# Transformer block on one core: attention products in bursts of sixteen matmuls, projection pieces between the two scores of a pair

## What is computed

```python
mod = (silu(c) @ wmod).reshape(8, 6, 1, 512)          # sa, ca, ga, sb, cb, gb; |ga|, |gb| >= 0.25
h = layernorm(x) * (1 + ca) + sa
q, k, v = ((h @ W + bias).reshape(b, 16, 32, 1024) for each)   # a plain reshape: 64 tokens make one head
attn = softmax(einsum('bhdt,bhds->bhts', k, v) * temperature)  # scores from k and v
x = x + ga * einsum('bhdt,bhts->bhds', q, attn).reshape(b, 1024, 512)
h = layernorm(x) * (1 + cb) + sb
x = x + gb * (h with, for the 512 tokens of the highest router score, sigmoid(score) * ffn(h) added)
```

## Time and profile before

| | |
|---|---|
| median of three runs | 2613.66 us |
| profiled execution, its own time | 2608.22 us |
| its span, first to last instruction | 2606.5 us |
| mean granted TensorE clock, as a share of 2.4 GHz | 0.971 |
| row maxima, L708 on DVE | 1024, 1216 ns each |
| Exp, L598 on ACT | 1024, 1117 ns each |
| qn, L769 on DVE | 257, 643 ns each |

### The profile page before, as it was taken

The page is one execution under the profiler, slowest core; times in us unless marked ns, Lnnn a source line. Parts: engine busy times, 40 slices in busy tenths (PEclk is TensorE's granted clock), DMA queues, the critical chain, the costliest instruction groups (busy, mean ns, idle before and its releaser), DMA issues. The chain is left out here.

```text
span 2606.5 us, 42013 instructions
## 1 busy us (share of the span) xinstructions
PE 2347.0 (90%) x13016; PEld 897.3 (34%) x13016; DVE 2014.1 (77%) x2697; ACT 1498.0 (57%) x2631; POOL 1247.9 (48%) x1103
## 2 busy tenths in 40 slices
PE   7899999999999999999999999991099999999996
PEld 2333333333333333333333333330044444444443
DVE  5899999899899999999999989994456446644632
ACT  1788788788788788878888878871211111111110
POOL 4455555455455545555455545552314535443541
PEclk9999999999999999999999999996599999999998
DMA  6322232232332232223223233226701120112010
GB/s 200 77 70 73 66 96 62 75 81 71 78 82 74 64 90 75 70 67 90 70 75 82 70 79 82 74 63 36 193 18 44 41 61 32 48 40 61 21 53 16
DMA packets 124912, 183.60 MB, mean 70 GB/s; under 512 B 43748, under 2 KB 43748, under 8 KB 124656
## 3 DMA queue, kind: packets, MB, share of 16 engines
q1 hardware_dynamic: 114936, 155.46, 24.5%
q0 software_dynamic: 9728, 25.23, 3.1%
HBM read 68.23 MB, written 43.16 MB: 43 GB/s over the span
## 5 line engine op out<-in xcount | busy, mean ns | idle before, releaser
L708 DVE TENSOR_REDUCE nmax<-sc 128x1 f32<-128x1024 f32 x1024 | 1230.1, 1216 | 131.9 <-PE sc L409 120.1
L598 ACT ACTIVATE probs<-sc,nmax 128x1024 f32<-128x1024 f32 x1024 | 1138.1, 1117 | 337.1 <-DVE nmax L708 319.4
L409 PE MATMUL sc<-stacks 128*128 128x512 f16 x2048 | 615.7, 382 | 80.3 <-ACT probs L598 47.0
L457 PE MATMUL acc<-probs,qn 128*32 128x512 f32 x4136 | 551.8, 606 | 9.8 <-DVE x L746 7.3
L1156 ACT ACTIVATE g<-ff,b_col 128x512 f32<-128x512 f32 x128 | 88.0, 687 | 578.8 <-PE ff L1095 528.4
L409 PEld LDWEIGHTS sc<-stacks 128*128 128x128 f16 x2048 | 155.1, 97 | 612.4 <-ACT probs L598 328.1
L1108 PE MATMUL ff<-w,g 128*128 128x512 f16 x1536 | 352.4, 379 | 14.7 <-DVE g L1205 13.9
L1095 PE MATMUL ff<-fT,w 128*128 128x512 f16 x1536 | 353.8, 381 | 1.6 <-DVE fT L1190 1.6
L1203 DVE CAST g<-g 128x512 f16<-128x512 f32 x128 | 76.9, 601 | 291.1 <-ACT g L1156 243.7
L887 POOL TENSOR_SCALAR k<-kv 128x512 f16<-128x512 f32 x66 | 41.0, 621 | 511.1 <-ACT kv L571 511.0
L1108 PEld LDWEIGHTS ff<-w,g 128*128 128x128 f16 x1536 | 148.8, 98 | 199.2 <-DVE g L1205 21.5
(11 more groups left out here) (127 smaller groups left out, 2178.1 us busy)
## 6 DMA issues: line engine op xcount, KB each, us to landing
stacks<-k SPq DMA_DIRECT2D x528, 64.0 KB, 2.0
stacks<-v SPq DMA_DIRECT2D x528, 64.0 KB, 2.0
xt<-in_L_attn_x SPq DMA_DIRECT2D x140, 128.0 KB, 2.6
h_rows<-hbuf SPq DMA_DIRECT2D x132, 128.0 KB, 2.3
out<-base SPq DMA_DIRECT2D x132, 128.0 KB, 2.5
rows<-mod_rows SPq DMA_DIRECT2D x32, 256.0 KB, 4.1
stage<-in_L_ffn_W SPq DMA_DIRECT2D x8, 1024.0 KB, 9.9
probs<-in_L_wmod SPq DMA_DIRECT2D x4, 1024.0 KB, 10.0
```

Of the source, the lines that this page charges most:

```text
L409: mm = nc.tensor.matmul(slot(g, v)[:, half * D:(half + 1) * D], stacks[g % 2][:, 0, hq, i * P:(i + 1) * P], stacks[g % 2][:, 1, hq, half * ...
L457: mm = nc.tensor.matmul(acc[at:at + DH, :], qn[:, (p // 2) % 2, p % 2, h2, :], probs[:, (2 * p + h2) % PROBS, half * D:(half + 1) * D], st ...
L598: nc.scalar.activation(probs[:, u % PROBS, :], slot(g, ring_at(p, h2)), ACT.Exp, bias=nmax[:, u % PROBS:u % PROBS + 1], accum_out=rsum[:, ...
L708: nc.vector.tensor_reduce(nmax[:, u % PROBS:u % PROBS + 1], slot(g, ring_at(p, h2)), AX.X, ALU.max, negate=True).then_inc(max_done, 1)
```

## The change

PE's order within a pair becomes: score tile 0, projection piece, score tile 1. Behind score tile 1 of every odd pair p the products of the pairs p - 3 and p - 2 follow as one burst of 16 matmuls. The wait for `qn` stands ahead of the burst, once for both, and so does the wait for the free accumulator (at p = 3 and 11, where it was at 4 and 12). The waits of the pieces for `kv_evac` and `q_evac` move with the pieces. The prologue's product counts 2 on `pv_done` where it counted nothing, since the burst of pair 1 now completes the pairs 14 and 15 of the group before. Behind the loop two pairs of products remain, not four. DVE reads `acc` at the pairs 2 and 10, where it did at 3 and 11.

```diff
-            products(NQ)
+            products(NQ).then_inc(pv_done, 2)
...
                         scores_of(b, g, p, 0)
-                        pe.wait_ge(qn_done, b * (GB * PAIRS // 2) + g * (PAIRS // 2) + p // 2 + 1)
-                        if p in (LAG, LAG + NQ):
-                            pe.wait_ge(acc_free, b * (GB * SUBS) + g * SUBS + (p - LAG) // NQ + 2)
-                        products((p - LAG) % PAIRS).then_inc(pv_done, 1)
-                        scores_of(b, g, p, 1)
                         if p < 12:
                             if p % 3 == 0:
...
                             whole(piece)
+                        scores_of(b, g, p, 1)
+                        if p % 2 == 1:
+                            pe.wait_ge(qn_done, b * (GB * PAIRS // 2) + g * (PAIRS // 2) + (p + 3) // 2)
+                            if p in (3, 3 + NQ):
+                                pe.wait_ge(acc_free, b * (GB * SUBS) + g * SUBS + p // NQ + 2)
+                            products((p - 3) % PAIRS).then_inc(pv_done, 1)
+                            products((p - 2) % PAIRS).then_inc(pv_done, 1)
...
-            for p in range(PAIRS, PAIRS + LAG):
-                pe.wait_ge(qn_done, B * (GB * PAIRS // 2) + (p - PAIRS) // 2 + 1)
-                products(p - LAG).then_inc(pv_done, 1)
+            pe.wait_ge(qn_done, B * (GB * PAIRS // 2) + 2)
+            for p in (PAIRS - 2, PAIRS - 1):
+                products(p).then_inc(pv_done, 1)
...
                         row_max(b, g, p, 0)
-                        if p == 3:
+                        if p == 2:
                             gated(b, g - 1, 1)
-                        if p == 11:
+                        if p == 10:
                             gated(b, g, 0)
```

## The result

The changed kernel takes 2785.31 us (median of 4 runs, 2782.34 to 2789.47) where the kernel before takes 2614.34: a ratio of 1.065 [1.063, 1.068]. The forecast was 2692, with a range of 2635 to 2750. It was slower, as forecast, but by 171 us and not by 78.

A forecast was written before the change was run, and what follows sets the result against it. PE was taken to bound ordinary pairs, the copies of v after the fourth evacuation the group's end. 2.44 us more in each of 32 groups, 78 us on 2608.2, gave 2686, scaled to the median 2692; range 2635 to 2750.

The forecast's parts named there:

- 95 or more: Sign of being right: PE's bias matmul waits for ACT's evacuation at p = 3 and 9, 95 us or more in all.
- piece 0 to piece 9: Group stretch from the projection piece of p = 0 to that of p = 9: 29.03 us against 26.74 before.
- p = 2, 3: Burst to burst over these pairs, with PE waiting 1.46 us for bank pj at p = 3: 7.30 us.
- p = 6, 7: Burst to burst over these pairs, with the piece starting at 2.99: 6.50 us, before 6.08.
- the piece of p = 9: Piece released after DVE's late statistics and aggregation delay the evacuation: 6.18 us from the start of the burst ahead.
- the rule on weight loads: Burst: loads run beside matmuls only if row groups differ; would cost some 0.2 more per burst, forecast some 40 us higher.
- rival 2: Much slower: qn comes late in most rounds because POOL holds it up; 2759 us, chance 0.13.
- the sum for one group: First score to fourth evacuation of an attention group: 40.42 us against 37.98, so 2.44 us more per group.
- From the first score to piece 0 it is 0.52: Start of a group: the first projection piece follows the first score by 0.52 us, where it was 2.07.
- the round of p = 4 and 5: Burst to burst over these two pairs: 5.54 us, before 5.66.
- Behind the fourth evacuation I keep the 15.11: End of a group: GpSimd split and DMA copies of v up to the next first score stay at 15.11 us.
- could cost up to 1 us a group: End of a group: extra cost if PE's and DVE's two rounds, 13.6 to 15 us, don't fit the 15.11.

The follow-up runs named there:

- the early evacuation: Changed kernel with each k/v slice in two pieces at the first two of its three pairs, evacuated in the second: 2614.0 us, ratio 1.002.
- the cut subtract: Changed kernel with GpSimd's subtract of 2.13 us cut into four instructions: 2733.76 us, ratio 1.047.
- two halves: Against the kernel before: merged bursts alone at the old place, 2626.1 us; pieces moved between the two scores alone, single products kept, 2672.24 us.

## Why the prediction missed the size

**What held.** The mechanism and its place: waits of the bias matmul of over 1 us at p = 3 and 9, 127.5 us in all where 95 or more were named, and a ratio of 1.002 where the early evacuation takes them away. Most rounds came out within 0.1 us of the working: piece 0 to piece 9 29.43 against 29.03, with p = 2, 3 at 1077.65 - 1070.26 = 7.39 (7.30 forecast), p = 6, 7 at 6.54 (6.50), and the piece of p = 9 at 6.17 behind its burst (6.18). The burst's 16 matmuls take the 1.92 of the earlier trace rows in the loop too, not 2 x 1.06, so the forecast was right to leave the rule on weight loads aside. The mean qn fell to 0.555 us, and PE waits for it in one place of a group only (p = 13): rival 2 was not what happened, though the time went beyond its 2759.

**What failed** is the sum for one group, the 2.44 us. From piece 0 to piece 0, the mean over 31 groups grew from 53.02 to 58.63, by 5.61 us, 174 in all. The terms, worked out for an ordinary group; the last row holds what the edges of a batch add to it:

| term, over 31 groups | us | shown by |
|---|---|---|
| forecast, 31 x 2.44 | 76 | early evacuation removes it |
| clock falls behind the stall at p = 9, 27 x 1.63 | 44 | matmuls added ahead of the stall remove it |
| clock falls in the first pieces of a batch, 7 x 1.6 | 11 | read in the trace only |
| first piece waits for `evac_q`, 0.43 in most groups | 13 | gone in most groups with the cut subtract |
| qn of p = 4 beside GpSimd, and small shifts, 0.43 a group | 13 | read in the trace only |
| the group of the earlier trace rows took 53.09, others 52.78 on average | 10 | trace of before |
| batch edges, 2.0 above other groups where it was 1.05 | 7 | not settled |

The largest missing term is the clock, 55 of the 98 us that the sum lacks. The sum had no term for it: it priced the stall of p = 9 at its own length and took every matmul behind it at full speed, though it was the forecast itself that put a stall of this size into PE's order. The Trainium skill, "TensorE: Matmul & The Clock Gate", section "HAM oscillation — how this bites in real kernels", says that a wait which comes back in every round can throttle TensorE anew in every round, so that the loss is paid each time. The trace agrees in this, with 28 falls in 32 groups; but the waits of the page's example are longer than the stall of 1.98 us behind which the clock fell here, and the measurement decides. A fall of the clock should have been among the rivals.

The second is the step "From the first score to piece 0 it is 0.52". It is 0.95, since piece 0 now also stands close behind its evacuation, that of q, and waits 0.35 for it. A third, smaller one is the round of p = 4 and 5, 5.82 where 5.54 was forecast: its qn takes 0.62 us beside another GpSimd instruction, the one that normalises the input, and with the subtract cut the round takes 5.80.

The step "Behind the fourth evacuation I keep the 15.11" came out at 15.13, but for another reason than the one given. The copies of v no longer end last; the burst's wait of 1.34 for the held qn, and PE's and DVE's rounds, fill the same time. The warning that this "could cost up to 1 us a group" had named the right place. With qn cut loose some 0.7 a group came back, and the DMA wait with it. So the hold is a cost that the old wait would in part have taken up.

On that hold the Trainium skill, "SBUF — State Buffer", section "Who interferes with whom", says that a VectorE instruction with two inputs in SBUF and a GpSimd instruction that reads SBUF exclude each other, the later one until the first ends, while a reduction never contends. The trace agrees: 2.08 us beside the whole subtract, 0.62 beside its quarters, and the row maximum at 1114.60 is not lengthened by the GpSimd work that starts at 1114.49 (2.34 for two, 2.33 in the earlier trace rows).

**What stays open.** At the edge of a batch PE stands still for 2.75 us ahead of the first score, labelled with an Exp that had ended 2.6 us before:

```profile
1006.60 0.60 PE L409 MATMUL sc<-stacks 128*128 128x512 f16 x2 [2.75 <-ACT probs L600]
```

Batch edges last longer than other groups by 1.05 us in the kernel before, 2.0 after, 2.3 to 2.4 in the two with the early evacuation alone or with the change; no run took the loop itself apart. (Falls of the clock are left out of these figures.) The trace has a candidate that no experiment took up. At the seven edges inside the loop, in the kernel before and in the changed one, a transfer of 16 KB starts on the queue that the page lists as `q8 instruction`, and the first score follows 2.7 to 3.3 us behind its start; ahead of no other group does one stand there. In the changed kernel it starts 0.5 us before PE falls idle, in the kernel before 0.7 to 1.4 us before. That fits a wait for instructions where the loop jumps back, but no run tests it. At the edge shown above, the window 1003.3 to 1004.8 holds one such transfer (packets, MB, share of the DMA engines' time in the window):

```profile
q8 instruction: 1, 0.02, 5.8%
```

Nor is it settled which falls of the clock the same stall of 1.98 us brings about: 28 of 32 in the changed kernel, 15 of 32 with the subtract cut.

## What to carry to other kernels

When an edit moves work nearer to the release of a shared buffer, walk the chain from score to evacuation with the trace's handovers: it gave the three waits of the k and v pieces here to 0.1 us, and it missed those of pieces 0, 12 and 14 (0.35, 0.40 and 0.72 us), for which it had not been walked. Then look at what stands behind each wait, since a stall of TensorE can also slow the matmuls that follow it. And if two halves of an edit each use up slack, time them alone: here 15 and 61 us became 171, and the cure, evacuating one pair earlier, lay in neither half.

## What the hardware showed that was not expected

- The clock fell behind a stall of 1.98 us and not, in the same group, behind one of 1.49. It cost 1.63 us over the next 3.57 us of work. Six matmuls issued for nothing in each group, ahead of the stall, made the changed kernel 45 us faster.
- The same stall of 1.98 us, at the same place, let the clock fall in some groups and not in others.
- A DVE multiply that takes 0.29 us undisturbed took 2.08 beside one GpSimd subtract, and 0.62 beside the same subtract in four parts, which took 2.62 in place of 2.13 us.
